# Opening of a fused Macaron layer: one layer-norm root per sequence, x and GpSimd work moved around it

## The reference, cut to what matters

```
x = x + 0.5 * ffn(layernorm(x))
x = x + mixer(layernorm(x))
x = x + 0.5 * ffn(layernorm(x))

ffn(x): x = fwht(x * SU_ug) / 64
        h = silu(x @ W_gate.T * s_gate) * (x @ W_up.T * s_up)      # 2048 wide
        h = fwht(h * SU_dp) / 64
        return h @ W_down.T * s_down
```

## Time and profile before

| | |
|---|---|
| three runs | 1642.84, 1643.42, 1644.26 us |
| profiled execution | 1645.84 us, of which 1644.0 us are the profile's span |
| TensorE busy | 1621.2 us, 99% of the span |
| TensorE's first matmul | 8.98 us |
| VectorE, ScalarE, GpSimd busy | 63%, 38%, 23% |

### The profile page before, as it was taken

How to read it: one execution, slowest core, us unless ns; L and a number is a source line. 1 busy time by engine, 2 the same in 40 slices (tenths; PEclk the granted TensorE clock), 3 DMA queues, 4 the chain that set the end, 5 groups by cost and what they waited for, 6 DMA issues and landing times.

```text
span 1644.0 us, 25044 instructions
## 1 busy us (share of the span) xinstructions
PE 1621.2 (99%) x9672; PEld 1313.0 (80%) x9672; DVE 1034.7 (63%) x2022; ACT 626.3 (38%) x934; POOL 378.9 (23%) x298
## 2 busy tenths in 40 slices
PE   6999999999999999999999999999999999999999
PEld 3788888878888778888787888877888878888887
DVE  6543445785677877777776768777775684543333
ACT  5333343464333463333454334355333341122111
POOL 1666652012212212122122122122122121000000
PEclk9999999999999999999999999999999999999999
DMA  9745654754444444454445444445444437556763
GB/s 325 275 172 212 231 192 172 263 183 149 164 163 160 144 156 150 151 169 157 143 162 162 158 152 159 157 131 194 156 156 157 156 127 224 167 181 191 215 203 129
DMA packets 252403, 290.46 MB, mean 177 GB/s; under 512 B 14464, under 2 KB 211200, under 8 KB 243072
## 3 DMA queue, kind: packets, MB, share of 16 engines
q1 hardware_dynamic: 252288, 288.88, 53.0%
HBM read 238.51 MB, written 50.33 MB: 176 GB/s over the span
## 4 chain that ended last, share of the span: by engine, by line
PE 74%; DVE 3%; ACT 1%; issue 1%; DMA 0%; SPq 0%; ACTq 0%; DVEq 0%
PE bank L1191 31%; PE bank L1232 14%; PE bank L1147 12%; PE bank L1260 5%; PE bank L1329 3%; PE bank L1300 2%; PE bank L1316 2%; PE bank L1278 2%; PE bank L1288 1%; PE bank L1323 1%; DVE xT L1750 0%; DVE res L1776 0%; DVE m_cv L1792 0%; DVE m_L L1823 0%; DMA cum_stay<-m_aS 0%
## 5 line engine op out<-in xcount | busy, mean ns | idle before, releaser
L1191 PE MATMUL bank<-fxT,wj 128*128 128x512 f32 x1752 | 415.2, 390 | 0.0
L1191 PEld LDWEIGHTS bank<-fxT,wj 128*128 128x128 f32 x1752 | 328.7, 188 | 68.5
L1232 PE MATMUL bank<-m_wd,m_hb 128*128 128x512 f32 x1128 | 278.8, 393 | 0.0
L1232 PEld LDWEIGHTS bank<-m_wd,m_hb 128*128 128x128 f32 x1128 | 209.2, 188 | 44.9 <-issue 2.4
L1544 ACT CAST m_hb<-xn 128x512 fp32r<-128x512 f32 x96 | 59.5, 620 | 452.5 <-DVE xn L1763 452.5
L1147 PE MATMUL bank<-xT,wi 128*128 128x512 f32 x900 | 224.4, 397 | 1.6 <-DVE m_cv L1792 0.5
L1147 PEld LDWEIGHTS bank<-xT,wi 128*128 128x128 f32 x900 | 167.2, 189 | 40.1 <-issue 5.1
L1776 DVE TENSOR_TENSOR res<-bank,res 128x512 f32<-128x512 f32 x192 | 132.5, 690 | 83.0 <-PE bank L1232 80.9
L2099 POOL TENSOR_TENSOR m_L<-m_L,m_GT 128x512 f32<-128x512 f32 x36 | 52.8, 1466 | 434.4 <-ACT m_L L1553 434.4
L1763 DVE SCALAR_TENSOR_TENSOR xn<-bank,sc,xn 128x512 f32<-128x512 f32 x96 | 71.7, 747 | 121.6 <-PE bank L1191 121.5
L1538 ACT ACTIVATE xn<-bank,sc 128x512 f32<-128x512 f32 x96 | 66.1, 689 | 146.3 <-PE bank L1191 140.9
(11 more groups left out here) (224 smaller groups left out, 2317.8 us busy)
## 6 DMA issues: line engine op xcount, KB each, us to landing
wj<-ug_split SPq DMA_DIRECT2D x167, 512.0 KB, 4.2
m_wd<-dn_split SPq DMA_DIRECT2D x48, 1024.0 KB, 4.8
wi<-in_split SPq DMA_DIRECT2D x76, 512.0 KB, 3.2
ug_split<-b_wu SPq DMA_DIRECT2D x8, 2048.0 KB, 14.0
m_wo<-out_split SPq DMA_DIRECT2D x32, 512.0 KB, 4.1
wi<-ug_split SPq DMA_DIRECT2D x25, 512.0 KB, 4.2
in_split<-b_msp SPq DMA_DIRECT2D x20, 512.0 KB, 3.8
raw<-in_wug SPq DMA_DIRECT2D x8, 1024.0 KB, 6.8
```

Of the source, the lines that this page charges most:

```text
L1191: ins = pe.matmul(to[:], w[:, a, k, :], frm[:, b, k, :], start=(k == 0 and i == 0), stop=(k == KH - 1 and i == 2))
L1232: ins = pe.matmul(F[t % 2][:], hb[:, a, j, ck(t)], wd[:, b, j, :], start=(j == 0 and n == 0), stop=(j == 1 and n == 2))
```

## The change

Five moves, all in `begin`:

1. SP issues x of the first sequence behind two group loads and not behind four.
2. VectorE makes the statistics and the root of sequence 0 alone (128x4 operands where there were 128x8). The statistics, root and bias of sequence 1 follow behind the low parts of the first turns and group 8.
3. TensorE and ScalarE do groups 2 and 3 behind the four turns of chunk 0. `rows(1)` waits for the second bias, and stands behind the copy of group 11.
4. VectorE scales groups 10 and 12 ahead of 4, 5, 6, 7, 9, 11, 13; groups 14 and 15 are still the last.
5. GpSimd scales groups 2 and 3 only after the first bias (`s_mv` 1), and starts the butterflies of chunk 1 after the second bias (`s_mv` 2), not after VectorE's last scaling (`s_gw` 8).

```diff
--- before.py
+++ after.py
@@ -346,9 +346,11 @@
                 sp.dma_start(group_tile(i), wdn[PQ * i:PQ * (i + 1)].rearrange("i (a n) -> (i a) n", a=FB)).then_inc(s_gl[i], 16)
 
             fetch(0)
-            for i in range(4):
-                load_group(i)
+            load_group(0)
+            load_group(1)
             sp.dma_start(res[:, 0:TPG, :], xt[:, 0:TPG, :]).then_inc(s_x0, 16)
+            load_group(2)
+            load_group(3)
             sp.dma_start(res[:, TPG:2 * TPG, :], xt[:, TPG:2 * TPG, :]).then_inc(s_x1, 16)
             sp.wait_ge(s_x0, 16)
             for i in range(4, 12):
@@ -430,9 +432,11 @@
 
             pool.wait_ge(s_par, 64)
             for i in range(4):
+                if i == 2:
+                    pool.wait_ge(s_mv, 1)
                 pool.wait_ge(s_gc, i + 1)
                 pool.tensor_tensor(group_tile(i), group_tile(i), wdp[:], ALU.mult).then_inc(s_gp, 1)
-            pool.wait_ge(s_gw, FB // 2)
+            pool.wait_ge(s_mv, 2)
             butterflies(1, False)
             butterflies(1, True)
             for c in range(NC):
@@ -552,11 +556,11 @@
 
             pe.wait_ge(s_par, 64)
             pe.wait_ge(s_c, 8)
-            for i in range(4):
-                group(i)
+            group(0)
+            group(1)
             for k in range(KH):
                 turn(("ug", 0, k))
-            for i in range(4, 8):
+            for i in range(2, 8):
                 group(i)
             for t in range(TPG):
                 turn(("x", 0, t))
@@ -606,7 +610,7 @@
 
             def rows(c, ts=range(TPG)):
 
-                act.wait_ge(s_mv, max(1, c))
+                act.wait_ge(s_mv, c + 1)
                 if c:
                     act.wait_ge(s_tm, turns["x", c - 1, TPG - 1] + 1)
                 for t in ts:
@@ -647,18 +651,19 @@
             act.wait_ge(s_par, 64)
             act.activation(s["acol"][:], pr[:, P_ALOG:P_ALOG + 1], ACT.Exp).then_inc(s_ex, 1)
             act.wait_ge(s_c, 8)
-            for i in range(4):
-                group(i)
+            group(0)
+            group(1)
             for k in range(KH):
                 turn(("ug", 0, k))
-            group(4)
-            group(5)
+            for i in range(2, 6):
+                group(i)
             rows(0)
             for t in range(TPG):
                 turn(("x", 0, t))
             group(6)
             group(7)
             group(9)
+            group(11)
             rows(1)
             act.wait_ge(s_sc, 16)
             def high_blocks(n):
@@ -671,7 +676,6 @@
                 keys = unit_turns(n)
                 silu(n, 0)
                 if n == 0:
-                    group(11)
                     group(13)
                 for key in keys[0]:
                     turn(key)
@@ -787,17 +791,22 @@
             dve.wait_ge(s_b0, 2)
             for n, op in enumerate((ALU.add, ALU.subtract)):
                 dve.tensor_tensor(raw[:, 0, 2 * n:2 * n + 2, :], t1[:, 0:2, :], t1[:, 2:4, :], op).then_inc(s_b0, 1)
-            for landed, c in ((s_x0, 0), (s_x1, 1)):
-                dve.wait_ge(landed, 16)
-                for t in range(TPG * c, TPG * c + TPG):
-                    own.done(dve.bn_stats(st[:, t, :], res[:, t, :]))
-            run(roots(dve, st, mv, own))
-            bias(0, 2 * TPG)
+            dve.wait_ge(s_x0, 16)
+            for t in range(TPG):
+                own.done(dve.bn_stats(st[:, t, :], res[:, t, :]))
+            run(roots(dve, st[:, 0:TPG], mv[:, :, 0:TPG], own))
+            bias(0, TPG)
             for k in range(KH):
                 turn(("ug", 0, k))
             for t in range(TPG):
                 turn(("x", 0, t))
-            for i in (8, 4, 5, 6, 7, 9):
+            group(8)
+            dve.wait_ge(s_x1, 16)
+            for t in range(TPG, 2 * TPG):
+                own.done(dve.bn_stats(st[:, t, :], res[:, t, :]))
+            run(roots(dve, st[:, TPG:2 * TPG], mv[:, :, TPG:2 * TPG], own))
+            bias(TPG, TPG)
+            for i in (10, 12, 4, 5, 6, 7, 9, 11, 13):
                 group(i)
             def low_blocks(n):
                 if n >= 2:
@@ -808,9 +817,6 @@
             third = stats(TPG, TPG, 2 * TPG)
             for n in range(UNITS - 1):
                 keys = unit_turns(n)
-                if n == 0:
-                    for i in range(10, 14):
-                        group(i)
                 for key in keys[0]:
                     turn(key)
                 if n == 0:
```

## The result

The changed kernel takes 1658.97 us (median of 4 runs, 1658.29 to 1660.12) against 1643.13 us of the kernel before (4 runs). The ratio is 1.0096, 95% interval 1.0078 to 1.0113: slower by about 16 us. The profiled executions differ by less, 14.3 us in the span (1658.3 against 1644.0 us).

The account below looks back on a forecast made before the run. TensorE, busy 99% of the span, was taken as the bound. Its turn starts 13.9 us later, plus 1.65 us of slow clock: 15.5 us on the 1643.42 median gives 1659, range 1649 to 1664.

Parts of the forecast that it names:

- First root: VectorE's statistics and root of sequence 0: bias at 19.7, 3.4 us earlier; first `up` at 26.9, gaining 2.5 us.
- The hole ahead of chunk 0's turns: TensorE idle 0.7 us between the end of groups 0 and 1 at 12.3 and chunk 0's turns at 12.93.
- Second root: VectorE's statistics, root and bias of sequence 1, behind the low parts and group 8, end at 34.15.
- Which products are held: VectorE products with two SBUF inputs wait beside a busy GpSimd; those with one input in a bank do not.
- Taking turns: From 34.2 on, each VectorE scaling with two SBUF inputs waits for one GpSimd product; one such round takes 2.81 us.
- `fetch(2)` in time: Chunk 2's data, issued at 37.6, lands at 44.3, about 1.2 us before GpSimd is free, so the alternation continues.
- The first rival: Alternation of GpSimd and VectorE ends after chunk 1 if `fetch(2)` lands after 45.5: 8.8 us, 1652; chance 0.16.
- Restart: TensorE, idle since 38.2, starts the turn at 54.85; slow clock after the hole adds 1.65 us.
- Behind it: After the late turn, the down weights' load stands at 65 at the latest, keeping its 4.3 us; nothing closer than before.
- no rounds: GpSimd does not hold VectorE's scalings; group 14 done at about 41, stores late: 4 to 5 us later, 1648; chance 0.11.

## Why the prediction was right

It was right in time (1659 forecast, 1658.97 measured) and in mechanism. By its steps:

- First root: bias forecast at 19.7, measured at 19.33; first `up` 26.9 against 26.44, without a slow stretch. The hole ahead of chunk 0's turns was 0.29 us and not 0.7.
- Second root: 34.15 against 33.56.
- Which products are held: as said, those with two inputs in SBUF. The bank reads at 33.47 and 52.97 took 0.68 beside a busy GpSimd, and the run with bank inputs shows it for the scalings themselves.
- Taking turns: seven scalings, seven GpSimd products, in strict alternation. The round was 2.75 us and not 2.81, and a scaling took 2.82 us and not 0.68. The rule of the Trainium skill, "SBUF — State Buffer", section "Who interferes with whom", holds here in both parts, the two inputs and the exclusive lock; the trace adds the order when both have a queue.
- `fetch(2)` in time: issued at 36.95, it took 5.4 us to land and not 6.7, so it was there at 42.4, two microseconds before GpSimd wanted it at 44.39. The first rival needed it after that.
- Restart: turn 53.70 against 54.85, and 1.5 us of slow clock against 1.65.
- Behind it: the loads of the down weights were forecast at 65 at the latest and were issued at 57.84, so the stores were further from setting the time than the forecast had them.

For the profiled executions 15.5 us were forecast and 14.3 were measured; 1.15 of the difference is the turn's start. The medians lie 15.8 apart. So the agreement to 0.03 us is partly luck: the profiled execution before lay 2.4 us above its median, the one after 1.2 above its own. Nothing in the opening explains this difference. The kernel before had medians of 1644.15 and 1644.38 us over 21 runs each beside the experiments; against these the changed kernel is 14.6 to 14.8 us slower, which is nearer to the spans than to the 15.8 from four runs, though it was not run again beside them.

The rival "no rounds" was priced at 4 to 5 us, from the store queue. The run with the wait put back is that case, and came out at 5.6. It named the down weights, and the run with the moved store shows that they cost 3.3 of it. So this second cost stands ready behind the first, as that rival had it: taking out the rounds does not bring the kernel back to 1643.

## What to carry to other kernels

Before one engine's work is started "earlier, in its idle time", look at what the other engine of the VectorE and GpSimd pair does there, and count its products with two inputs in SBUF: each waited for the rest of a GpSimd product, so 0.7 us became 2.8, and behind seven of them TensorE went on 13.2 us later (53.70 against 40.50). Give the two engines either different stretches or operands in a bank, or give GpSimd the contested products themselves. And when work is moved behind something on one engine, follow the transfers that wait for it: here they cost 3.3 us, about what the earlier root had gained at the first `up` (3.0).

## What the runs showed of the hardware

- Alternation was strict over seven rounds: the engine that waited went next, though the other had its next product ready. Order of issue would give the same there, and one place in the kernel before speaks for it, where VectorE's small steps have two inputs in SBUF as well. The one at 471.81 starts 0.02 us ahead of GpSimd's product and was not held, although VectorE had just had a turn (the step of 470.64); the one at 471.88 starts behind it and was held to its end. This is a single place, and starts on GpSimd are rough:

```profile
471.81 0.15 DVE L163 TENSOR_TENSOR m_mv<-m_st 128x4 f32<-128x4 f32 x1
471.83 1.28 POOL L2120 TENSOR_TENSOR m_yh<-m_y,m_yh 128x512 fp32r<-128x512 f32 x1
471.88 1.25 DVE L164 TENSOR_TENSOR m_mv<-m_st 128x4 f32<-128x4 f32 x1
```

- The same hole does not always cost clock. After 2.93 us idle at 37 to 40 the clock stayed at 1.00 in the run with bank inputs (`up` behind it 3.04 us); after 2.95 and 2.93 us in the two runs with the wait put back it fell to 0.50 for 3.4 us (`up` 3.78 and 3.99 us). TensorE's order of work ahead was the same in all three, its times within 0.4 us. What decides it stays open. In the run with bank inputs:

```profile
42.00:43.00 1.00, 1.00 (x6) 0.82 (x5) 0.90 (x2) 0.07 (x1) 1.00 (x1) 1.00 1.07 410
```

and in the run with GpSimd's wait put back:

```profile
42.00:43.00 1.00, 1.00 (x5) 0.90 (x4) 0.69 (x1) 0.73 (x2) 1.00 (x1) 0.50 1.06 408
```
